# An earlier, pipelined start of the first MLP, and a quarter of the key blocks moved to ScalarE

## What is computed

```python
# layer 0: self attention, cross attention, MLP; 16 heads of 16
def attention(q, k, v, mask):
    scores = einsum('bhqd,bhkd->bhqk', q, k) / sqrt(16)
    scores = scores * mask - 10000.0 * (1.0 - mask)
    return einsum('bhqk,bhkd->bhqd', softmax(scores), v)
x = x + merge(attention(split(ln1(x) @ w_qkv + b_qkv), ltor_mask)) @ w_ao + b_ao
x = x + merge(attention(ln2(x) @ w_q + b_q, ctx @ w_kv + b_kv, cross_mask)) @ w_co + b_co
x = x + gelu_tanh(ln3(x) @ w1 + b1) @ w2 + b2           # w1: 256 x 1024
# layer 1: per batch of x and ctx (64 channels x 256)
Mn, Mm = Wn @ inorm(x) + bn, Wm @ inorm(ctx) + bm
A = softmax(Mn^T Mm);  x = Wo @ ((Wl @ ctx + bl) A^T) + bo + x
# layer 2: two cross attentions with 16 heads of 128, an MLP; layer 3: a recurrent block
```

## Time and profile before

| | |
|---|---|
| time, median of 3 runs | 988.94 us (987.16 to 989.01) |
| profiled execution | 988.11 us, span 986.3 us |
| busy share of the span | PE 96%, PEld 81%, DVE 60%, ACT 46%, POOL 42% |
| granted TensorE clock, mean | 0.998 |

### The profile page before, as it was taken

One profiled execution on the slowest core, in us unless ns is written; L12 is line 12 of the kernel. 1 busy time (PEld: TensorE's weight loads), 2 busy tenths in 40 slices (PEclk: granted clock), 3 DMA queues, 4 the chain that ended last, 5 costly groups with the idle time before them and its releaser, 6 DMA issues.

```text
span 986.3 us, 21444 instructions
## 1 busy us (share of the span) xinstructions
PE 942.9 (96%) x8324; PEld 794.5 (81%) x8324; DVE 595.7 (60%) x972; ACT 450.3 (46%) x993; POOL 413.5 (42%) x572
## 2 busy tenths in 40 slices
PE   6999998998999999999999999999999999999998
PEld 4777776976788889988897888998888888678776
DVE  5999995767644433444356443344426766999883
ACT  4566674238643343333434333333342434576565
POOL 3242355965365433423246443332422862344331
PEclk9999999999999999999999999999999999999999
DMA  9100000310011111111101110111100100000000
GB/s 303 31 23 2 3 1 17 120 54 1 2 55 49 53 34 41 37 48 53 54 8 55 49 53 21 37 53 48 53 21 19 38 17 1 1 2 6 12 7 23
DMA packets 24147, 37.15 MB, mean 38 GB/s; under 512 B 4432, under 2 KB 16528, under 8 KB 23824
## 3 DMA queue, kind: packets, MB, share of 16 engines
q1 hardware_dynamic: 24080, 36.23, 11.8%
HBM read 35.17 MB, written 1.05 MB: 37 GB/s over the span
## 4 chain that ended last, share of the span: by engine, by line
PE 69%; DVE 14%; POOL 5%; issue 5%; ACT 5%; DMA 1%; SPq 0%; DVEq 0%; POOLq 0%; ACTq 0%
PE ps L1250 18%; PE ps L757 12%; PE ps L1267 9%; PE ps L1309 6%; PE ps L1906 5%; PE ps L1285 4%; PE ps L855 2%; DVE sb L634 2%; PE ps L1295 2%; DVE sb L628 2%; DVE sb L2434 1%; ACT sb L1690 1%; POOL sb L804 1%; PE ps L1984 1%; POOL sb L806 1%
## 5 line engine op out<-in xcount | busy, mean ns | idle before, releaser
L804 POOL TENSOR_TENSOR sb<-sb 128x256 fp32r<-128x256 f32 (+1 forms) x128 | 102.5, 801 | 286.2 <-DMA sb<-in_heads_a 151.3
L1250 PE MATMUL ps<-sb 128*128 128x512 f32 x768 | 187.7, 396 | 1.0 <-issue 1.0
L1250 PEld LDWEIGHTS ps<-sb 128*128 128x128 f32 x768 | 139.5, 188 | 33.0 <-ACT sb L1383 3.1
L757 PE MATMUL ps<-sb 128*128 128x256 f32 x1152 | 148.7, 286 | 0.8 <-DVE sb L901 0.7
L757 PEld LDWEIGHTS ps<-sb 128*128 128x128 f32 x1152 | 141.3, 191 | 3.7 <-issue 1.7
L806 POOL TENSOR_TENSOR sb<-sb 128x256 fp32r<-128x256 f32 (+1 forms) x128 | 116.3, 909 | 10.0
L1480 DVE SCALAR_TENSOR_TENSOR sb<-ps,sb 128x512 fp32r<-128x512 f32 x64 | 45.1, 746 | 96.2 <-ACT sb L1416 96.2
L1267 PE MATMUL ps<-sb 128*128 128x256 f32 x768 | 99.2, 285 | 0.4 <-DVE sb L1448 0.4
L1460 DVE TENSOR_REDUCE sb<-ps 128x8 f32<-128x520 f32 x32 | 22.4, 700 | 126.6 <-PE ps L1285 126.6
L1267 PEld LDWEIGHTS ps<-sb 128*128 128x128 f32 x768 | 95.0, 191 | 3.0 <-issue 0.9
L1383 ACT ACTIVATE sb<-ps,sb 128x512 f32<-128x512 f32 x64 | 43.8, 684 | 107.9 <-PE ps L1250 107.8
(11 more groups left out here) (217 smaller groups left out, 1655.6 us busy)
## 6 DMA issues: line engine op xcount, KB each, us to landing
sb<-in_heads_a SPq DMA_DIRECT2D x32, 386.0 KB, 3.0
sb<-in_heads_c SPq DMA_DIRECT2D x16, 256.0 KB, 3.6
sb<-in_heads_b SPq DMA_DIRECT2D x32, 128.0 KB, 3.0
sb<-in_mlp_a SPq DMA_DIRECT2D x16, 128.5 KB, 2.0
sb<-in_mlp_b SPq DMA_DIRECT2D x16, 128.0 KB, 2.1
sb<-in_w_r SPq DMA_DIRECT2D x1, 2048.0 KB, 7.8
sb<-in_encT SPq DMA_DIRECT2D x1, 1024.0 KB, 7.0
sb<-in_ctx SPq DMA_DIRECT2D x1, 1024.0 KB, 7.6
```

The lines of the kernel that those rows point to most:

```text
L757: last = pe.matmul(m.acc(t), lhsT[x], rhs[w], start=opens and n == 0, stop=False, skip_group_check=True)
L804: pool.tensor_tensor(high, src, one, ALU.mult).then_inc(*G.did(name + "_high", u))
L1250: last = pe.matmul(m.ps[u][:, c, :], m.w_parts[u][w][:, (KD * q + k) * P:(KD * q + k + 1) * P], rows[x][:, k, c * 512:(c + 1) * 512], star ...
```

## The change

Two things. First, the key blocks f = 1, h = 0 and 1 (2 of 8) are made by ScalarE as Identity(x * headmask column + key_bias column), where key_bias is made once by VectorE from headmask and the key bias; VectorE makes the other six, with a wait for ScalarE's before its own. Second, the first MLP's order FIRST replaces PLAIN: fc1(0, 0, 0) and fc1(1, 0, 0) go into slots 16 and 17 in place of keep-warm matmuls, their Gelus and the split of the first into slot 17, fc2 of u and fc1 of c = 0, r = 1 into slot 18, and the rest alternates first- and second-layer pieces. A tiny activation behind the last exp calls Gelu first. GpSimd's splits for r = 1 move ahead of the last row work, and its list in the MLP is reordered to match. In the second layer heads_qk_gpsimd moves behind the norm, one stream per slot in slots 0 and 1, and seven keep-warm matmuls are added in slot 3.

```diff
+OWN = 2
@@ attn0_tensor
     def warm(now, n):
         if now:
             pe.wait_ge(m.s_h[0], 4)
-            keep_warm(pe, m.x0, m.h_parts[0][:, 0, 0:512], n)
+            pe.wait_ge(*done["mul"].at(len(ITEMS) - 1))
+            keep_warm(pe, m.y[:, 1, :], m.h_parts[0][:, 0, 0:512], n)
...
         if slot == SLOTS - 1:
-            for u, free in enumerate((done["qT"], done["pT1"])):
-                pe.wait_ge(*free.at(len(ITEMS) - 1))
-                fc1(pe, ph, m, 4, u, 0, 0)
-                if u == 0:
-                    turn_rows(slot - 3)
-        if slot < SLOTS - 1:
-            turn_rows(slot - 3)
+            fc2(pe, ph, m, 0, 0, 0)
+            fc1(pe, ph, m, 4, 0, 0, 1)
+        turn_rows(slot - 3)
         keys(slot)
-        warm(slot == SLOTS - 3, 6)
-        warm(slot == SLOTS - 2, 4)
+        if slot in (SLOTS - 3, SLOTS - 2):
+            u = slot - (SLOTS - 3)
+            pe.wait_ge(*(done["qT"], done["pT1"])[u].at(len(ITEMS) - 1))
+            fc1(pe, ph, m, 4, u, 0, 0)
...
+    fc2(pe, ph, m, 1, 0, 0)
+    fc1(pe, ph, m, 4, 1, 0, 1)
@@ attn0_scalar
+    def keys(i):
+        act.wait_ge(*done["k"].at(i))
+        act.wait_ge(m.s_masks, 1)
+        if i >= 2:
+            act.wait_ge(*done["scores"].at(i - 2))
+        for h in range(OWN):
+            bias = HB * ATTN0.index(ITEMS[i][0]) + h
+            last = act.activation(m.kdiag[i % 2][:, 1, h, :], m.x1[:, P:2 * P], ACT.Identity,
+                                  bias=m.key_bias[:, bias:bias + 1], scale=m.headmask[:, h:h + 1])
+        last.then_inc(*m.own_act.did("keys", i))
...
         rows(slot)
+        if slot == SLOTS - 2:
+            gelu_rows(act, ph, m, ACT.Gelu_apprx_tanh, 0, 0, 0)
         mlp_rows(slot - 3)
-        if slot == SLOTS - 1:
-            for u in range(STREAMS):
-                gelu_rows(act, ph, m, ACT.Gelu_apprx_tanh, u, 0, 0)
+        keys(slot)
         context(slot - 2)
+        if slot == SLOTS - 2:
+            gelu_rows(act, ph, m, ACT.Gelu_apprx_tanh, 1, 0, 0)
         query(slot)
         exp(slot - 1)
+        if slot == SLOTS - 3:
+            act.activation(m.bv[0][:, :], m.col("eps"), ACT.Gelu_apprx_tanh)
@@ attn0_vector
-        for f in range(KD):
+        vec.wait_ge(*m.own_act.at("keys", i))
+        for f, first in ((0, 0), (1, OWN)):
+            n = HB - first
...
+        if slot == SLOTS - 2:
+            mlp_split(vec, ph, m, 0, 0, 0)
         add(slot - 2)
+    mlp_split(vec, ph, m, 1, 0, 0)
@@ attn0_gpsimd
+        if slot == SLOTS:
+            split_fc1(pool, ph, m, 0, 1, streams=(1,))
         row_split(slot - 4)
+        if slot == SLOTS - 1:
+            split_fc1(pool, ph, m, 0, 1, streams=(0,))
         row_rstd(slot - 3)
...
-PLAIN = [(kind, c, r) for r in range(MLP_ROUNDS) for kind in ("fc1", "fc2") for c in range(2)]
+EARLY = 3
+FIRST = [("fc1", 0, 0), ("fc2", 0, 0), ("fc1", 0, 1), ("fc1", 1, 0), ("fc2", 0, 1), ("fc2", 1, 0), ("fc1", 1, 1), ("fc1", 0, 2),
+         ("fc2", 1, 1), ("fc1", 1, 2), ("fc2", 0, 2), ("fc2", 1, 2), ("fc1", 0, 3), ("fc1", 1, 3), ("fc2", 0, 3), ("fc2", 1, 3)]
...
+def mlp0_gpsimd(pool, ph, m):
+    split_fc2(pool, ph, m, 0, 1)
+    split_fc1(pool, ph, m, 0, 2)
+    split_context_gpsimd(pool, m, 0, 4)
+    split_fc2(pool, ph, m, 0, 2)
+    context_norm_gpsimd(pool, m)
+    split_fc1(pool, ph, m, 0, 3)
+    split_context_gpsimd(pool, m, 4, 8)
+    split_fc2(pool, ph, m, 0, 3)
@@ inorm_tensor
+        if slot == 3:
+            warm(7, m.n_ps)
@@ inorm_gpsimd
-        if slot == 0:
-            heads_qk_gpsimd(pool, hd, m, 4, 0, 0, free["w"](0))
         rstd(slot)
         normed(slot)
-        if slot == 0:
-            heads_qk_gpsimd(pool, hd, m, 4, 1, 0, free["w"](1))
+        if slot in (0, 1):
+            heads_qk_gpsimd(pool, hd, m, 4, slot, 0, free["w"](slot))
```

More of the change, by code:

```diff
@@ L608, in keys @@
             vec.wait_ge(*done["scores"].at(i - 2))
-        for f in range(KD):
+        vec.wait_ge(*m.own_act.at("keys", i))
+        for f, first in ((0, 0), (1, OWN)):
+            n = HB - first
             last = vec.scalar_tensor_tensor(
-                out=m.kdiag[i % 2][:, f, :, :], in0=bc(m.x1[:, f * P:(f + 1) * P], 1, [P, 4, P]),
-                scalar=m.col("bk_" + ITEMS[i][0], f), in1=bc(m.headmask[:, :], 2, [P, 4, P]), op0=ALU.add,
+                out=m.kdiag[i % 2][:, f, first:HB, :], in0=bc(m.x1[:, f * P:(f + 1) * P], 1, [P, n, P]),
+                scalar=m.col("bk_" + ITEMS[i][0], f), in1=bc(m.headmask[:, first:HB], 2, [P, n, P]), op0=ALU.add,
                 op1=ALU.mult)
@@ L681, in attn0_vector @@
         if slot == 0:
+            vec.wait_ge(m.s_head, 16)
+            for n, kind in enumerate(ATTN0):
+                vec.tensor_scalar(m.key_bias[:, HB * n:HB * (n + 1)], m.headmask[:, :], m.col("bk_" + kind, 1), None, ALU.mult)\
+                    .then_inc(*m.own_vec.did("key_bias", n))
+            vec.wait_ge(*m.own_vec.at("key_bias", len(ATTN0) - 1))
             masks(0)
             vec.wait_ge(m.s_masks, 1)
-            vec.wait_ge(m.s_head, 16)
         if slot == 4:
@@ L806, in split_gpsimd, with split_fc1 @@
     pool.tensor_tensor(low, src, high.bitcast(F32), ALU.subtract).then_inc(*G.did(name, u))
-def split_fc1(pool, ph, m, loads, r, free=None):
-    for u in range(STREAMS):
+def split_fc1(pool, ph, m, loads, r, free=None, streams=range(STREAMS)):
+    for u in streams:
         high, low = (x[:, r % 2 * KD * P:(r % 2 + 1) * KD * P] for x in m.w_parts[u])
@@ L876, in mlp_tensor @@
                 fc2(pe, ph, m, u, c, r)
-            elif r or c or not begun:
+            else:
                 fc1(pe, ph, m, rows_split, u, c, r)
@@ L885, in gelu_rows, with mlp_scalar @@
                    bias=m.wm(u, r)[:, KD * P:KD * P + 1]).then_inc(*ph.act.did(f"gelu{c}", u))
-def mlp_scalar(act, ph, m, gelu, begun, steps):
+def mlp_scalar(act, ph, m, gelu, steps):
     for kind, c, r in steps:
         for u in range(STREAMS):
-            if kind == "fc1" and (r or c or not begun):
+            if kind == "fc1":
                 gelu_rows(act, ph, m, gelu, u, c, r)
@@ L911, in mlp_vector, with mlp2_gpsimd @@
             context_norm_vector(vec, m, r)
-def mlp_gpsimd(pool, ph, m, loads, rounds, first):
+def mlp0_gpsimd(pool, ph, m):
[7 more added lines that the diff above has]
+    split_fc2(pool, ph, m, 0, 3)
+def mlp2_gpsimd(pool, ph, m, loads, rounds):
     for r in rounds:
@@ L917, in mlp_gpsimd @@
         split_fc2(pool, ph, m, loads, r)
[L918 to L921, removed]
 def add_half(vec, m, c):
@@ L1641, in first_heads, with warm @@
                 head_product(pe, hd, m, "k", 1, c, 0, [done["pT1"].at(TILES - 1)])
-    def warm(n):
-        keep_warm(pe, m.pT_ps[:, 0, :], m.enc_parts[0][:, 0, 0:512], n)
+    def warm(n, bank=m.pT_ps[:, 0, :]):
+        keep_warm(pe, bank, m.enc_parts[0][:, 0, 0:512], n)
     pe.wait_ge(m.s_split, 8)
@@ L2907, in _ @@
             attn0_gpsimd(pool, ph["mlp0"], m)
-            mlp_gpsimd(pool, ph["mlp0"], m, 0, range(1, MLP_ROUNDS), True)
+            mlp0_gpsimd(pool, ph["mlp0"], m)
             inorm_gpsimd(pool, heads[1], m, free[1])
@@ L2944, in _ @@
             seam_scalar(act, ph["norm3"], None, m, "wm_s", "wm_b")
-            mlp_scalar(act, ph["mlp2"], m, ACT.Gelu, False, HALVES[:-LATE])
+            mlp_scalar(act, ph["mlp2"], m, ACT.Gelu, HALVES[:-LATE])
             rwkv_scalar(act, m, ph["mlp2"])
```

22 lines of the change are left out of this document (12 added, 10 removed).

## The result

The changed kernel takes 984.69 us (median of 6 runs, 982.93 to 986.47) against 989.54 us (median of 6, 987.16 to 990.31) for the kernel before: ratio 0.9948, 95% interval 0.9933 to 0.9963. It is faster by 0.5%, 4.9 us; 981.3 was forecast, with a range of 977.8 to 985.3. Two slow executions further down, one of the kernel before (1043.62 us, mean clock 0.85) and one of the run without key blocks (1297.99 us, 0.652), are left out of the ratios and move the medians given by at most 0.1 us. The profiled execution took 984.63 us, its span is 982.8 us, the mean clock 0.995.

The account below looks back on a forecast made before the run. VectorE was taken as nearly full in steady attention slots, TensorE in the first MLP. 2.0 - 0.8 + 6.65 - 0.65 = 7.2 us off 988.11 gave 980.9, with half an offset given back 981.3; range 977.8 to 985.3.

Parts of the forecast that it names:

- Part 3: First MLP: fewer waits and matmuls already done cut 49.95 us to 43.3, 6.65 us won; bounds 7.5 and 3.
- the last seven pairs: First MLP, lower bound: VectorE at 1.9 us per split holds each of these by 0.5, leaving 3 us won.
- Part 2: Last three attention slots: added matmuls cost 0.46 us, the early Gelu table load makes ScalarE 0.34 late; 0.8 us lost.
- Part 1: First attention's slots: two key blocks on ScalarE save VectorE 0.27 us per item; 2.0 us won in all.
- a ring over ScalarE: Slots 2, 3, 5, 7: value rows, keys, new pair, context copies, output matmul, scores set the length; gain 0.07 us.
- self slots shorten to 8.3 us: First attention, sign against the forecast, which had slots of the self kind still 8.5 us long.
- Part 4: Second layer's start: first projection 0.8 us sooner, but third norm and added keep-warm matmuls delay scores; net 0.65 us lost.
- My bound of 1.5 lost: Second layer's start: the worst case, 1.5 us lost if GpSimd's list takes a tenth longer.
- Rival 1: Second layer's start costs nothing and wins its 0.8 us: 979.8, down to 978 with more of Part 1; chance 0.17.
- Rivals 2 and 5: Attention slots: ScalarE last in all, 983.8, chance 0.13; or context copies delayed 0.72 us in each slot, 995, chance 0.04.
- rival 3: First MLP: VectorE holds TensorE back, so Part 3 gives only 3 us: 985; chance 0.10.
- The other signs: Trace marks: table load near 150, MLP's end near 200, first project under 2 us behind it, VectorE waiting only in slot 0.

Follow-up runs that it names:

- keys alone: The kernel before with only the two key blocks moved to ScalarE: 988.13 us, ratio 0.9987 to the kernel before.
- the base: The changed kernel with GpSimd's split of the heads' value weights moved behind the third tile's norm: 980.32 us, and 981.23 us when timed again.
- items 1 to 12: The base with ScalarE's two key blocks only for items 1 to 12, VectorE making all eight of the others: 979.19 us, ratio 0.9892.

## Why the prediction was right, and where it was off

The direction and the range held; the time came 3.4 us above the forecast, near its upper end. By steps:

**Part 3, 6.65 us won: 6.63, the last digit by luck.** 43.3 us were said and 43.32 measured. The wait of 0.39 us before the transposes and the 0.19 for them are the 0.6 that was said. But the 0.5 us set aside for VectorE never came, TensorE not idling at all from 162 us on, and the first- and second-layer matmuls took 42.74 us, not 42.2, which fills the same gap. (With no wait the bound would have been 49.95 - 42.2 = 7.75, not 7.5.) That VectorE keeps ahead only because pieces alternate was right too (without it 47.05 us, part of that by the clock), though I had put the danger on the last seven pairs, and it is in the first rounds.

**Part 2, 0.8 us lost: 0.41.** The load with its activation delays the copies from 152.81 to 153.10, 0.29 us, of which 0.07 was there before; 0.34 was said. The activation takes 0.10 us till the next starts, not 0.25. There is nothing beside the load's 1.28 us, so the trace does not agree with the drain that the Trainium skill, page "ScalarE: Activation LUTs", section "What ACT_TABLE_LOAD costs", adds to a switch, here either. The matmuls cost 0.25 us, not 0.46: from the start of the six to L409 are 1.48 us (155.08 to 156.56), where I had counted the 1.73 of a group that something waits for at its end; the four took 1.23. Without the early load it would have been 0.76 us worse.

**Part 1, 2.0 us won: size nearly right, the slots wrong.** Between slot 1 and the scores of slot 16 the five traces with ScalarE's blocks and no clock fall there take 121.74 to 121.87 us (121.79 keys alone, 121.81 the base again and items 1 to 12), 2.8 us less than before. I had 0.43 us for slots 2, 3, 5, 7 and 9 together, through a ring over ScalarE, where 1.0 was measured, and said that I would be wrong where self slots shorten to 8.3 us. From key pair to key pair they did, 8.31 in the changed kernel. The ring does close on TensorE: in slots 2, 3, 5 and 7 the scores are 8.50 or 8.51 apart in the base's second trace (46.94 to 55.44 in slot 5), with ScalarE's copies right behind the new pair. What I missed is the slot behind: in slot 6 VectorE's product runs 1.46 us and not the 1.68 of slot 5, and the next scores are 8.13 behind. The mean of the two is what VectorE sets, so the 0.07 us per ring slot was no loss of VectorE's gain but a delay of it. Slot 0's loss of 0.5 was right: from its keys to its scores 3.34 us in the base, 2.77 before. By medians 1.3 us (keys alone, taken from before; 0.4 to 2.2 by the interval) and 1.75 us (left out of the change) remain of the 2.0.

In the profiled pair none of it is seen, for three things outside it: the clock fall at 20 to 25 us (9.83 us from slot 1 to 2, 8.32 in the second trace of the base, 1.5 us); the keys of slot 0, which came at 9.46 before and at 9.75 now; and VectorE's first product, 1.23 us before and 1.72 here. That product meets an operation of GpSimd's, which took 1.61 us before and 0.72 in the base: one of the two pays. In the one execution of before that I had to read all three fell well, and it was 1.4 us below the median of the six.

**Part 4, 0.65 us lost: 3.3 lost. This is the step that failed.** The price of the reordered GpSimd list was too low, and so was that of what follows. The MLP's end to the end of the third norm was 14.9 us, not 13.9: GpSimd starts 0.14 us behind the MLP's end and not 0.3 before it, for VectorE's statistics came later, and the list took 14.74 us. Before it took 14.4, and I had put 14.2 without a reason. In it one split took 1.59 us instead of 0.61 beside VectorE, where before the third norm had taken 1.85 instead of 1.22. Before, the first split began in idle time, 1.72 us ahead of the MLP's end; moved behind the norm, it lengthened what follows the MLP. The projection was done at 17.5, not 15.3, because it ran at the lower clock behind its own wait of 2.71 us (2.58 us from 216.69 to the seven at 219.27, against 1.33 in the run without key blocks, whose clock stayed up). The seven took 2.08, not 1.65. In sum 1.0 + 1.2 + 0.4 = 2.6 us more. In a trace without the clock fall (without key blocks) it is 18.08 us, a loss of 1.8. My bound of 1.5 lost, a list longer by a tenth, held no clock, and was short by its own terms: a tenth of 14.4 on top of 0.65 is 2.1. The 16.3 us of before were a draw as well: in the run with the key blocks alone, whose second layer is that of before, the weights landed sooner, the list began 2.32 us ahead of the MLP's end, and the third tile's scores stood 15.69 us behind it. That what this stage loses does reach the end was right: moving two splits out of the way gave 3 to 4 us.

So by measured terms: part 1 1.5, part 2 -0.4, part 3 6.6, part 4 -3.3, together 4.4, beside 4.9 measured. The terms come from single traces, and some 1.5 us of part 4 are the clock's, which not every execution pays. Rival 1 (the start costs nothing, 979.8) was wrong for the kernel as changed; with the value weights moved it is near what came out, 980.3 and 981.2. Rivals 2 and 5 are shut out by the key pairs, rival 3 by 43.32 us; rival 3's mechanism is real, since it came up when the order did not alternate.

The other signs: the first project came 2.08 us behind the MLP, not under 2, and the third late with ScalarE waiting for it, as said. No wait of VectorE's for ScalarE but in slot 0 was wrong for slots 14 and 15 (0.79 us each, of no cost) and, behind the clock fall, slot 2. The table load near 150 came at 151.70; the MLP's end near 200 at 201.75, the difference being part 1's.

## What to carry to other kernels

When a stage ends sooner, read the in-order list of every engine that feeds the next one, and ask what in it is not needed for the first tile that waits; here two weight splits ahead of a norm gave back half of what a better matmul order had won. Another split placed early, beside VectorE's last work, cost 3 us in another way, so ask as well who runs beside it. A wait of TensorE's can cost more than its length, so give it a second price too, the matmuls behind it at the lower clock. One profile of before is one draw: compare the same interval in several traces before a term of 1 us is believed or given up.

## What the runs showed of the hardware

The granted clock fell in single stretches at a few places, and not in every execution. From 15 to 25 us it was down, to 0.54 to 0.83 of a 5 us stretch, in seven of the twelve experiments' traces and in the changed kernel's, and 1.00 in the other five. Such a share is the 1.2 GHz level for a part of the stretch: groups of matmuls took 1.97 us for 1.09, or 1.06 for 0.61. Ahead of falls TensorE had been idle (1.91 us at 20.88, 2.71 at 216.69, 2.08 at 205.87, 1.98 at 215.27, 1.94 at 169.14), but idle time of the same length also left the clock up. The 1.90 to 1.92 us ahead of the second item's scores (near 21 us) stand in nine traces: in five the clock fell there, in four it didn't. And 2.71 and 2.72 us at the third norm left it up in the runs without key blocks and without the seven. From slot 1 to 2 a fall cost 0.8 us (without key blocks) to 1.9 us (without the seven), ahead of the fourth tile 1.4. The two fastest of the changed kernel's six runs (982.93 and 983.19 us) had a mean clock of 0.998, the other four 0.994 or 0.995.

GpSimd and VectorE slow each other where their operations meet, and which of the two pays changes from trace to trace: 1.23 or 1.72 us for the same product on VectorE with 1.61 or 0.72 for GpSimd's beside it, and 0.26 to 1.34 for GpSimd's small L224 in slot 15. Four context norms of VectorE's took 3.16 us beside a weight split and 1.38 without it.
